# Joining neighbouring networks at four stage borders of a one-core block kernel (attention, two mixtures of experts, router)

## The reference, cut to what matters

```
def cond(x, t):        # first mixture: a shared gated network and one expert per sequence
    share  = (gelu(x @ sWi0) * (x @ sWi1)) @ sWo
    expert = (gelu(x @ Wi0[t]) * (x @ Wi1[t])) @ Wo[t]
    w = softmax(relu(concat(expert[:, 0], share[:, 0]) @ g0) @ g1)
    return expert * w[0] + share * w[1]
def cond2(x, t):       # second mixture: three shared networks, two experts per sequence
    s_j   = relu(x @ share_wi[j]) @ share_wo[j]                 # j = 0, 1, 2
    out_a = relu(x @ expert_wi[t])   @ expert_wo[t]
    out_b = relu(x @ expert_wi[t+1]) @ expert_wo[t+1]
    expert = out_a * wa + out_b * wb
    g = softmax(relu(concat(expert[:, 0], s_0[:, 0], s_1[:, 0], s_2[:, 0]) @ gate_w1) @ gate_w2)
    return expert * g[0] + s_0 * g[1] + s_1 * g[2] + s_2 * g[3]
x = x + causal_attention_16_heads(cond(x, type))
x = x + routed_top2_ffn_8_experts(cond2(x, type))
```

## Time and profile before

| | |
|---|---|
| median of three runs | 2357.82 us (2357.38 to 2362.7) |
| the profiled execution's own time | 2358.76 us |
| its span in the trace | 2357.2 us |
| PE busy | 2284.8 us, 97% |
| DVE busy | 1140.3 us, 48% |
| ACT busy | 1083.5 us, 46% |
| POOL busy | 328.5 us, 14% |
| mean granted TensorE clock | 0.993 |

### The profile page before, as it was taken

How to read it: one execution, slowest core, us unless ns; L and a number is a source line. 1 busy time by engine, 2 the same in 40 slices (tenths; PEclk the granted TensorE clock), 3 DMA queues, 4 the chain that set the end, 5 groups by cost and what they waited for, 6 DMA issues and landing times.

```text
span 2357.2 us, 52378 instructions
## 1 busy us (share of the span) xinstructions
PE 2284.8 (97%) x19327; PEld 1486.6 (63%) x19328; DVE 1140.3 (48%) x2332; ACT 1083.5 (46%) x2072; POOL 328.5 (14%) x486
## 2 busy tenths in 40 slices
PE   5999999999999999999999999999999999989998
PEld 2444488887787444444445888888444444458886
DVE  5554355445998542332323444454344445444444
ACT  3554354444888442332323444443344444446663
POOL 0000000011564100000000111110000000004556
PEclk9999999999999999999999999999999999989999
DMA  4231011012444430120111333342211111012434
GB/s 126 87 104 60 28 50 36 19 33 71 107 111 89 140 107 36 54 80 28 38 42 41 117 120 116 104 139 73 77 36 37 36 36 36 36 54 74 116 98 128
DMA packets 165861, 171.94 MB, mean 73 GB/s; under 512 B 99476, under 2 KB 143508, under 8 KB 156724
## 3 DMA queue, kind: packets, MB, share of 16 engines
q1 hardware_dynamic: 138740, 80.15, 11.6%
q0 software_dynamic: 21168, 74.11, 9.5%
q10 hardware_dynamic: 5776, 15.25, 2.1%
HBM read 107.57 MB, written 50.86 MB: 67 GB/s over the span
## 4 chain that ended last, share of the span: by engine, by line
PE 94%; DVE 1%; DMA 1%; ACT 1%; issue 1%; SPq 1%; POOL 0%; ACTq 0%; POOLq 0%; DVEq 0%
PE ps L833 33%; PE ps L883 26%; PE ps L1166 14%; PE ps L1285 4%; PE ps L1297 4%; PE ps L1155 4%; PE ps L788 3%; PE ps L1016 1%; PE ps L1073 1%; PE ps L1180 1%; PE ps L1027 1%; PE ps L1064 1%; PE ps L1043 0%; DMA misc<-in_x 0%; PE ps L978 0%
## 5 line engine op out<-in xcount | busy, mean ns | idle before, releaser
L833 PE MATMUL ps<-xh,arena 128*128 (+1 forms) x5376 | 888.8, 308 | 23.4 <-DVE xh L1790 15.2
L883 PE MATMUL ps<-misc,arena 128*128 128x256 f16 (+2 forms) x4128 | 712.0, 308 | 5.9 <-DVE misc L2011 2.6
L833 PEld LDWEIGHTS ps<-xh,arena 128*128 (+1 forms) x5376 | 514.6, 98 | 292.6 <-issue 30.3
L883 PEld LDWEIGHTS ps<-misc,arena 128*128 (+1 forms) x4128 | 394.9, 98 | 218.9 <-issue 5.5
L2011 DVE SCALAR_TENSOR_TENSOR misc<-ps,misc 128x256 f16<-128x256 f32 (+1 forms) x464 | 248.1, 535 | 489.2 <-ACT misc L1421 487.3
L1421 ACT ACTIVATE misc<-ps 128x256 f16<-128x256 f32 (+1 forms) x464 | 219.0, 472 | 519.1 <-PE ps L833 518.9
L1166 PE MATMUL ps<-arena 128*128 128x512 f16 x1536 | 337.2, 379 | 0.0
L1166 PEld LDWEIGHTS ps<-arena 128*128 128x128 f16 x1536 | 148.0, 98 | 172.9
L2276 DVE TENSOR_TENSOR arena<-misc,arena 128x512 f16<-128x512 f32 x128 | 88.6, 692 | 229.2 <-ACT arena L1589 229.2
L2005 DVE TENSOR_TENSOR arena<-ps,misc 128x256 f32<-128x256 f32 (+1 forms) x200 | 101.7, 508 | 136.5 <-ACT misc L1417 135.7
L1588 ACT ACTIVATE misc<-ps,bias 128x512 f32<-128x512 f32 x128 | 87.8, 686 | 172.5 <-PE ps L1166 162.7
(11 more groups left out here) (312 smaller groups left out, 2063.0 us busy)
## 6 DMA issues: line engine op xcount, KB each, us to landing
wstage<-in_m_w POOLq DMA_DIRECT2D x16, 1024.0 KB, 5.7
parts_d<-misc POOLq DMA_DIRECT2D x64, 256.0 KB, 2.5
arena<-src_d SPq DMA_DIRECT2D x64, 256.0 KB, 3.8
src_d<-misc SPq DMA_DIRECT2D x24, 512.0 KB, 3.1
arena<-parts_d ACTq DMA_DIRECT2D x12, 1024.0 KB, 8.0
wstage<-in_c_wi POOLq DMA_DIRECT2D x6, 1024.0 KB, 5.4
wstage<-in_r_w POOLq DMA_DIRECT2D x5, 1024.0 KB, 5.5
cshare_d<-misc SPq DMA_DIRECT2D x8, 512.0 KB, 3.1
```

Of the source, the lines that this page charges most:

```text
L833: last = mm(ps[:, bank, col + c0:col + c0 + width], weight(p, off, half, g, wp, k * F + f * 128), xh[:, xp, k, ds(start, width)], start=(k ...
L883: last = mm(ps[:, 4 + 2 * half + m, c0:c0 + width], weight(p, off, half, 2 if p.gated else 1, wp, f * D + m * 128), hid[:, st % 4, hp, c0: ...
```

## The change

Four borders are changed: `cs` to `ce`, `s0` to `s1`, `s1` to `s2`, `s2` to `ee`. In the last steps of the network that ends, PE issues the `first` of the one that follows between its last calls of `second`; the follower's registers are loaded at step 11 of the last iteration; the last evacuation and the last feature copy stand at steps 1 and 3 of the follower, as between iterations. The functions `evacuate`, `feature` and `at_chunk` get the network as an argument and are otherwise as they were.

```diff
+        def behind(p):
+
+            return {"cs": ce, "s0": es[1], "s1": es[2], "s2": ee}.get(p.name)
...
             def ffn(p):
-                if p is cs:
-                    pe.wait_ge(s["perm"], 1)
-                elif p is not es[0]:
-                    pe.wait_ge(s["w_ready"], p.need_w)
-                if p is ce:
-                    pe.wait_ge(s["consts"], 1)
-                prev = before(p)
-                if prev is not None:
-                    pe.wait_ge(prev.ev, prev.nev)
...
+                prev, follower = before(p), behind(p)
...
                     if f == 0 and not (isinstance(i, int) and i == 0):
                         pe.wait_ge(p.ev, (i + p.i0) * 2 + (half - 1))
+                    elif f == 0 and prev is not None:
+                        pe.wait_ge(prev.ev, prev.nev - 1 + half)
...
                         if st == 11 and not lastone:
-                            ahead = pair_place() if to_pair else at_chunk(i + 1, 0)
+                            ahead = pair_place() if to_pair else at_chunk(p, i + 1, 0)
+                        if st == 11 and lastone and follower is not None:
+                            pe.wait_ge(s["consts"], 1)
+                            ahead = at_chunk(follower, 0, 0)
+                            if follower.dynamic:
+                                carry(ahead)
                         second(i, st, place[st // FC])
...
                         elif not lastone:
                             first(p, i + 1, nxt - 16, ahead)
+                        elif follower is not None:
+                            if nxt == n_st:
+                                pe.wait_ge(s["w_ready"], follower.need_w)
+                            first(follower, 0, nxt - n_st, ahead)
+                            if p.lead < follower.lead and st == n_st - 1:
+                                first(follower, 0, follower.lead - 1, ahead)
...
-                place0 = at_chunk(0, 0)
-                if p.dynamic:
-                    carry(place0)
-                for st in range(p.lead if p is not es[0] else 0):
-                    first(p, 0, st, place0)
+                if p is cs:
+                    pe.wait_ge(s["perm"], 1)
+                    for st in range(p.lead):
+                        first(p, 0, st, at_chunk(p, 0, 0))
...
                         if st == 1 and not first:
-                            evacuate(i - 1, 1)
+                            evacuate(p, i - 1, 1)
+                        elif st == 1 and before(p) is not None:
+                            evacuate(before(p), before(p).iters - 1, 1)
...
-                evacuate(p.iters - 1, p.last_steps // FC - 1)
+                if behind(p) is None:
+                    evacuate(p, p.iters - 1, p.last_steps // FC - 1)
...
                         if st == 3 and not first:
-                            feature(i - 1, 1)
+                            feature(p, i - 1, 1)
+                        elif st == 3 and before(p) is not None:
+                            feature(before(p), before(p).iters - 1, 1)
...
-                evacuate(p.iters - 1, p.last_steps // FC - 1)
-                feature(p.iters - 1, p.last_steps // FC - 1)
+                if behind(p) is None:
+                    evacuate(p, p.iters - 1, p.last_steps // FC - 1)
+                    feature(p, p.iters - 1, p.last_steps // FC - 1)
```

More of the change, by code:

```diff
@@ L897, in body @@
                     else:
-                        place = [at_chunk(i, 0)] * 2
+                        place = [at_chunk(p, i, 0)] * 2
                     n_st = p.last_steps if lastone else 16
@@ L1430, in x1_high @@
                 fn(xh[:, 0, :, ds(c * CH, CH)], x1, ACT.Copy, scale=SX).then_inc(s["x1_hi"], 1)
-            def ffn(p):
[L1433 to L1457, removed]
@@ new lines, in evacuate @@
+            def evacuate(p, i, half):
+                act.wait_ge(p.l2, (i + p.i0) * 2 + (half + 1))
+                if half == 0 and isinstance(i, int) and i == 0 and before(p) is not None:
+                    act.wait_ge(before(p).st, 16 * before(p).nst)
+                if p.two_experts:
+                    if half == 0:
+                        if not (isinstance(i, int) and i == 0):
+                            act.wait_ge(p.st, i * 16)
+                        act.wait_ge(s["consts"], 1)
+                        if i < NFULL:
+                            fn(outb[:, :, 0:p.n], ps[:, 4:6, 0:p.n], ACT.Copy,
+                               scale=wab[:, 0, i:i + 1]).then_inc(p.ev, 1)
+                        else:
+                            fn(outb[:, :, 0:CP], ps[:, 4:6, 0:CP], ACT.Copy, scale=wab[:, 0, i:i + 1])
+                            fn(outb[:, :, CP:CH], ps[:, 4:6, CP:CH], ACT.Copy, scale=wab[:, 0, i + 1:i + 2]
+                               ).then_inc(p.ev, 1)
+                    return
+                if p is cs and i == 0 and half == 0:
+                    act.wait_ge(s["consts"], 1)
+                if p is es[0] and i == 0 and half == 0:
+                    act.wait_ge(s["x1_lo"], NA)
+                if not (isinstance(i, int) and i == 0 and half == 0):
+                    act.wait_ge(p.st, (i + p.i0) * 32 + 16 * half)
+                fn(outb[:, :, 0:p.n], ps[:, 4 + 2 * half:6 + 2 * half, 0:p.n], ACT.Copy,
+                   scale=1 / SO).then_inc(p.ev, 1)
@@ new lines, in feature @@
+            def feature(p, i, half):
+                if p.dynamic and i == p.iters - 1 and (half == 1 or not p.two_experts):
+                    places = [dve.value_load(tbl[0:1, T_POS + NFULL + h:T_POS + NFULL + h + 1], min_val=0, max_val=B)
+                              for h in range(2)]
+                if p.two_experts:
+                    if half == 0:
+                        return
+                    dve.wait_ge(p.ev, i * 2 + 2)
+                else:
+                    dve.wait_ge(p.ev, (i + p.i0) * 2 + (half + 1))
+                nb = p.n // S
+                if p.dynamic and i == p.iters - 1:
+                    for h, b0 in enumerate(places):
+                        last = v.tensor_copy(gate_in[:, p.feat, :, ds(b0, nb // 2)], outb[:, :, h * CP:(h + 1) * CP:S])
+                        if h == 0:
+                            link(last)
+                    last.then_inc(p.feat_done, 1)
+                    return
+                if p.dynamic:
+                    c = i if p.two_experts else i * 2 + half
+                    b0 = dve.value_load(tbl[0:1, ds(c + T_POS, 1)], min_val=0, max_val=B)
+                else:
+                    b0 = (i * 2 + half) * nb
+                v.tensor_copy(gate_in[:, p.feat, :, ds(b0, nb)], outb[:, :, 0:p.n:S]).then_inc(p.feat_done, 1)
```

72 lines of the change are left out of this document (24 added, 48 removed).

## The result

The changed kernel takes 2347.59 us (median of five runs, 2344.97 to 2348.19) against 2358.23 us before (five runs, 2357.38 to 2362.7). The ratio of the runs is 0.9943 with a 95% interval from 0.9932 to 0.9954, that is 13.4 us less (10.9 to 16.0). The difference of the medians alone is 10.6 us. A second measurement of the same pair gave 2345.66 against 2360.05 us, ratio 0.9946 (0.9933 to 0.996), 12.7 us. `first` is L837 there, `second` L881, the evacuation L1463, the gelu L1425.

What follows compares the result with a forecast made beforehand. PE, busy 97% of the span, was taken to bound the kernel, so only its idle and half-clock time could be won: 4.35 + 2.74 + 4.69 = 11.78 us, from 2357.82 to 2346.0 us, range 2343.0 to 2350.5.

Steps and rivals of the forecast that it cites:

- The gap at `cs` to `ce`: Around the last `second` of `cs`: 4.71 us of PE gaps, 4.35 us won, 0.36 us left.
- The `s` borders: `s0` to `s1` and `s1` to `s2`: PE gaps of 1.365 and 1.375 us, all won, 2.74 us together.
- The border to `ee`: `s2` to `ee`: 2.985 us of gap and 1.71 us of half clock behind it, 4.69 us won.
- The clock: Half clock behind the gap at `s2` to `ee`: 1.71 us counted as won there, nothing at `cs` to `ce`.
- The rival that left the fall out: Gaps close, but the clock's fall was absent from the median runs or stays: gain 10.07 us, 2347.8 us; chance 0.14.
- The edits at nothing: Register loads, weight waits, moved evacuation, last store and feature copy at the borders: covered by other work, costing nothing.
- The rival of a gain given back by attention: Attention behind `ce`: its start doesn't move, 4.35 us come back; with uncovered loads too, 2354.0 us; chance 0.10.
- The slower rival: Attention behind `ce`: clock falls to half in a busy stretch, up to 23.4 us more, 2369 us; chance 0.04.

Runs made afterwards that it cites:

- the third trace of the kernel before: The kernel before, unchanged, traced again to see whether the clock falls behind the gaps of `cs` to `ce` and `s2` to `ee`; no time given.

## Why the prediction was right

It said 2346.0 us (2343.0 to 2350.5), faster; measured were 2347.59 and 2345.66. What was forecast is a gain of 11.78 us, and by the ratios it was 13.4 and 12.7. That the time itself was hit within 2 us is partly luck: 29 other executions of the kernel before have a median of 2361.19 us, 3.4 us above the 2357.82 from which the prediction counted down.

- The gap at `cs` to `ce`: forecast 4.35 us with 0.36 us left, found 4.43 and 0.36 (the 0.1 us by which the open block of `first` is longer than three calls was not in the sum). The hidden value of step 0 didn't hold up PE, as worked out.
- The `s` borders: forecast 1.37 and 1.37, found 1.37 and 1.36.
- The border to `ee`: forecast 4.69, found 4.69 in this pair of traces. That is the same trace of the kernel before from which the forecast was read, with its fall of the clock; it confirms that nothing new waits, not how large the term is on average.
- The clock is the term that was mis-sized. I took 1.71 us at `ee` and nothing at `ce`, from the one trace. Six executions show 1.0 us on average at `ee` and 1.2 us at `ce`, so 2.2 us for a mean and 12.3 us for the whole, where 11.78 stood. The traces read directly agree: from the second-to-last `second` of `cs` to the first of `ce` six open borders take 12.43 us on average and the joined one 6.90, and from the third-to-last `second` of `s2` to that of step 1 of `ee` 11.21 against 7.16, with 2.7 us of the `s` borders that makes 12.3 us. The two errors nearly cancel, which is luck. The rival that left the fall out (10.07 us, 2347.8 us) can't be told from the forecast by the medians, 2347.59 being nearer to it; by the mean over the traces it is 2.2 us short.
- The edits at nothing: the loads cost nothing, at step 11 or later. The evacuation had to move: with the one on ACT undone, 4.7 us come back in the traces. In its new place it delays no `second`; step 2 of `ce` had its value at 285.35 + 0.43 = 285.78 and ran at 286.98, 1.2 us to spare where I had 0.9.
- The rival of a gain given back by attention: 0.8 us went between `ce` and the middle of `s0` in this pair of traces, by a fall of the clock in the first steps of `s0` that the third trace of the kernel before shows at the same place. The stage before it takes 208.6 us on average in four traces of the kernel before and 208.25 in two of the changed one, so nothing was given back there; the variants scatter up to 214.1 us, and 1 or 2 us could not be told. The slower rival did not occur.

## What to carry to other kernels

At a border between two pipelined stages look for the same pattern as inside a stage: the next one's first products between the last ones that wait for another engine, and on that other engine the closing work behind the next one's first values. Both halves are needed; PE's order alone left 4.7 of some 12 us behind, and nearly all of what the two borders between like networks give. Count the time behind a gap along with the gap, over several traces, since the same gap costs more in some executions than in others.

## What the runs showed of the hardware

A PE gap of constant length (2.8 to 2.9 us idle) was followed by a granted clock of 0.50 (1.2 instead of 2.4 GHz) in four of six executions at each of two places, and not always in the same execution at both. At a third place, the first `second` of `s0`, waits of 2.5 to 3.1 us in eleven traces were followed by such a fall in four, which cost 1.1 to 1.4 us. With idle matmuls in the gap the clock stayed at 1.00 in the one trace taken, and the kernel with its gaps otherwise as they were was 5.4 us (3.1 to 7.8) faster. Behind the `s` borders, idle for 1.2 us, no trace shows a fall. The Trainium skill ("TensorE: Matmul & The Clock Gate", part 1) says that the monitor behind the clock runs free of the kernel's start; six traces agree with that, one could not show it.
